# Six LayerNorms of a two-layer decoder: the inverse root moves from ScalarE and VectorE to GpSimd

## The reference

```python
def _layernorm(x, axis=-1, eps=1e-05):
    m = jnp.mean(x, axis=axis, keepdims=True)
    v = jnp.var(x, axis=axis, keepdims=True)
    return (x - m) / jnp.sqrt(v + eps)
...
    x = _layernorm(x + _L0_attn_ref(x, ...), axis=-1)
    x = _layernorm(x + _L0_xattn_ref(x, ctx_2048, ctx_2048, L0_xattn_gamma), axis=-1)
    x = _layernorm(x + _L0_ffn_ref(x, ...), axis=-1)
    x = _layernorm(x + _L1_attn_ref(x, ...), axis=-1)
    x = _layernorm(x + _L1_xattn_ref(x, itok_BxS_13_99985, ...), axis=-1)
    x = _layernorm(x + _L1_ffn_ref(x, ...), axis=-1)
```

## Time and profile before

| | us |
|---|---|
| median of three runs (1048.7 to 1051.43) | 1048.94 |
| the profiled execution's own time | 1048.75 |
| its span, first to last instruction | 1047.0 |
| PE busy in the span | 842.6 |
| DVE busy | 625.5 |
| ACT busy | 439.3 |
| POOL busy | 433.7 |

### The profile page before, as it was taken

The page is one execution under the profiler, slowest core; times in us unless marked ns, Lnnn a source line. Parts: engine busy times, 40 slices in busy tenths (PEclk is TensorE's granted clock), DMA queues, the critical chain, the costliest instruction groups (busy, mean ns, idle before and its releaser), DMA issues. The chain is left out here.

```text
span 1047.0 us, 16284 instructions
## 1 busy us (share of the span) xinstructions
PE 842.6 (80%) x4838; PEld 498.2 (48%) x4838; DVE 625.5 (60%) x1971; ACT 439.3 (42%) x1422; POOL 433.7 (41%) x343
## 2 busy tenths in 40 slices
PE   1959998577475699889999998995994499999920
PEld 0445556344254344355555554883444355555510
DVE  0369994566558477668888887113665633433427
ACT  0038782355156100078888886001112155555512
POOL 0348871244026066556666664000000455565523
PEclk9989998677579699989999999998995599999975
DMA  9200000000000077620000000005911022222114
GB/s 349 108 1 1 0 1 1 0 2 1 0 1 1 17 164 171 141 81 1 2 1 2 1 1 1 1 1 212 317 74 40 16 63 71 73 69 70 51 57 144
DMA packets 30974, 60.44 MB, mean 58 GB/s; under 512 B 6465, under 2 KB 20429, under 8 KB 30032
## 3 DMA queue, kind: packets, MB, share of 16 engines
q1 hardware_dynamic: 17424, 35.99, 10.8%
q10 hardware_dynamic: 8864, 13.00, 4.4%
q0 software_dynamic: 4608, 10.50, 3.2%
HBM read 40.59 MB, written 8.39 MB: 47 GB/s over the span
## 5 line engine op out<-in xcount | busy, mean ns | idle before, releaser
L534 POOL TENSOR_TENSOR a_Pr<-a_Pr,a_rd 128x1024 f32<-128x1024 f32 x64 | 121.3, 1895 | 68.0 <-DVE a_rd L475 67.7
L507 ACT ACTIVATE a_Pr<-a_Sm,a_nm 128x257 f32<-128x257 f32 x256 | 127.3, 499 | 34.2 <-DVE a_nm L459 33.4
L459 DVE CUSTOM_DVE_ANT_0 a_Sm<-a_psS,table,NSK 128x256 f32<-128x256 f32 x256 | 107.7, 477 | 1.8 <-PE a_psS L408 1.8
L408 PE MATMUL a_psS<-KT,QT 64*128 64x256 f32 x512 | 74.2, 410 | 5.7 <-DVE a_nm L459 3.8
L1427 POOL TENSOR_TENSOR ro_in_tile<-ro_in_tile,table 128x384 fp32r<-128x384 f32 x4 | 7.0, 1746 | 173.0 <-DVE ro_in_tile L1486 173.0
L1597 POOL DMA_INDIRECT pairs<-ex_y,ti_index x48 | 49.6, 1034 | 57.5 <-ACT ex_y L1702 56.9
L1110 PE MATMUL p_ps<-p_XT,W 128*128 128x512 f32 x160 | 72.6, 612 | 0.8 <-ACT p_XT L1123 0.8
L408 PEld LDWEIGHTS a_psS<-KT,QT 64*128 64x128 f32 x512 | 45.3, 190 | 57.9 <-issue 48.6
L1140 DVE SCALAR_TENSOR_TENSOR p_T<-p_ps,BQK,table 128x512 f32<-128x512 f32 x80 | 56.4, 746 | 26.7 <-PE p_ps L1110 26.7
L1720 DVE TENSOR_TENSOR ex_a<-ex_psG,ex_sg 128x96 f32<-128x96 f32 x48 | 12.4, 258 | 99.9 <-ACT ex_sg L1690 99.9
L421 PE MATMUL a_psT<-table,a_Pr 128*128 128x128 f32 x512 | 70.8, 282 | 1.5 <-ACT a_PT L514 1.5
(11 more groups left out here) (265 smaller groups left out, 2001.2 us busy)
## 6 DMA issues: line engine op xcount, KB each, us to landing
w_in<-in_w_in SPq DMA_DIRECT2D x1, 6144.0 KB, 18.3
QT<-p_E SPq DMA_DIRECT2D x64, 64.0 KB, 2.1
QT<-p_E ACTq DMA_DIRECT2D x64, 64.0 KB, 2.1
c_in<-in_c_in SPq DMA_DIRECT2D x1, 4096.0 KB, 29.2
co_G<-pairs SPq DMA_DIRECT2D x8, 512.0 KB, 7.5
W<-in_w ACTq DMA_DIRECT2D x1, 3072.0 KB, 16.6
w_out<-in_w_out SPq DMA_DIRECT2D x1, 3072.0 KB, 43.0
KT<-p_E SPq DMA_DIRECT2D x32, 64.0 KB, 2.1
```

What stands on the lines that cost most here:

```text
L408: last = nc.tensor.matmul(psS[:, 2 * (t % 2) + u, qt, :], heads.q(g, n, qt), heads.k(g, n), start=True, stop=True, skip_group_check=True)
L459: nc.vector.tensor_tensor_reduce(out=Sm[:, t % 2, n, 0:S], in0=psS[:, 2 * (t % 2) + n // 2, n % 2, :], in1=mask[:, n % 2, :], scale=-scale ...
L507: nc.scalar.activation(Pr[:, t % 4, n, :], src, ACT.Exp, bias=nm[:, t % 2, n:n + 1], scale=scale if mask is None else -1.0, accum_out=den[ ...
L534: pool.tensor_tensor(p, p, rd[:, t % 2, :].unsqueeze(2).to_broadcast([P, 4, S]), ALU.mult).then_inc(normed, 1)
```

## The change

`Norm.root` is no longer run by ACT but by POOL, as two instructions of 128x8: variance plus epsilon into std, then, behind a wait for its own first instruction, std to the power of a column that holds -0.5 into rstd. Both are tensor_tensor with the second operand a column that is repeated along the row. DVE's reciprocal, and the wait between it and the first normalised tile, go away. The column with -0.5 is a new last column of the constants' table, which is loaded once at the start and grows from 2608 to 2609 columns. Which engine calls `root` is changed in all six users; the rest of the program is the same, but that tiles allocated behind the constants lie 32 bytes further on.

```diff
-    def root(self, act):
-        act.wait_ge(self.has_var, 1)
-        self.nc.scalar.activation(self.std[:, :], self.mv[:, :, 1], ACT.Sqrt,
-                                  bias=self.eps[:, 0:1]).then_inc(self.has_std, 1)
+    def root(self, pool):
+        pool.wait_ge(self.has_var, 1)
+        pool.tensor_tensor(self.std[:, :], self.mv[:, :, 1], self.eps[:, 0:1].to_broadcast([P, NT]),
+                           ALU.add).then_inc(self.has_std, 1)
+        pool.wait_ge(self.has_std, 1)
+        pool.tensor_tensor(self.rstd[:, :], self.std[:, :], self.power[:, 0:1].to_broadcast([P, NT]),
+                           ALU.pow).then_inc(self.has_std, 1)
 
     def apply(self, dve, out):
-        dve.wait_ge(self.has_std, 1)
-        self.chain.link(self.nc.vector.reciprocal(self.rstd[:, :], self.std[:, :]))
+        dve.wait_ge(self.has_std, 2)
...
-        @block.scalar
-        def _(act):
-            ln.root(act)
+        @block.gpsimd
+        def _(pool):
+            ln.root(pool)
...
-             sin0=S, causal=2 * S, window=2 * S, cos1=S, sin1=S, eps=1)
+             sin0=S, causal=2 * S, window=2 * S, cos1=S, sin1=S, eps=1, power=1)
...
-        cos1=cos1, sin1=sin1, eps=np.full((P, 1), EPS))
+        cos1=cos1, sin1=sin1, eps=np.full((P, 1), EPS), power=np.full((P, 1), -0.5))
```

More of the change, by code:

```diff
@@ L557, in __init__ @@
         self.eps = consts["eps"]
+        self.power = consts["power"]
         self.has_var = st.sem(name + "_has_var")
```

## The result

The changed kernel takes 1063.77 us (median of four runs, 1060.85 to 1064.98), the kernel before beside it 1050.18. The ratio is 1.0122 with a 95% interval of 1.0089 to 1.0155: the change makes the kernel slower by about 13 us. The profiled execution is the fastest of the four, 1060.85 us; its span is 1058.8.

A forecast was written before the change was run, and what follows sets the result against it. PE carries most of the span, but short stretches in the six norms with all engines but one idle decide. +5.1 for six norms and -1.28 at a1 sum to +3.8 us: 1052.7 as median, range 1047.5 to 1064.

The forecast's parts named there:

- a power dearer than 1.90 us: Rival: the power costs more than anything POOL does here; at 3 us a norm, +15.5 and 1064.3 us; chance 0.19.
- The six stretches: Last variance to first normalised tile in each norm, other engines idle: 0.61 us becomes 1.46, +0.85 each, +5.1 for six.
- The addition: POOL's 128x8 addition of variance and epsilon in each norm, wholly on the path: 0.20 us.
- the hand-overs: Between engines in each norm: DVE to POOL 0.08 us, POOL to itself 0.08, POOL to DVE 0.05.
- The loads ahead of the roots: Five ACT table loads for the root stand ahead of the wait for the variance: removing them is worth nothing.
- The load at a1: ACT's exponential table load at the second attention's start, behind DVE's first nm, is on the path: removing it gives -1.28 us.
- the rival that rested on it: A table switch costs more than its load, so a1 gains 2.66 us instead of 1.28: 1051.3 us; chance 0.03.
- a first power that pays for its code: Rival: the first power alone is held up by some microseconds, say 6, giving 1058.6 us; chance 0.04.
- The power: POOL's 128x8 power in each norm, on the path: 1.05 us, the middle of 0.20 and 1.90; break-even at 0.41.
- the cheap power: Rival: the power is about as cheap as an addition, 0.41 us or less; at 0.20, 1047.5 us; chance 0.12.
- Whatever is added to or taken from this stretch moves the whole program by as much, six times.: In all six norms DVE has nothing else to do between variance and first tile, so +0.85 us a norm gives +5.1.
- the shifted tiles: Later tiles lie 32 bytes further on: counted as zero, but blamed if a stage between norms ran at another speed.

The follow-up runs named there:

- filled wait: Changed kernel plus five 128x256 matmuls of constants on PE in te, while PE waits for the first tile's gate: 1060.54 us, ratio 1.0124 against the kernel before.
- the wider table: Kernel before with only the 2609th column added to the constants' table, norms as before: 1051.28 us against 1050.03, ratio 1.0011.
- the table loaded ahead: Kernel before plus a one-element exponential on ScalarE in the second projection's block, loading a1's table early: 1047.53 us against 1048.25, ratio 0.9997.
- the version with the filled wait and the early load: Kernel before with tile-by-tile GpSimd power in o0, ff, o1, te, a1's table loaded ahead, five matmuls in te's wait: 1041.17 us against 1050.44.

## Why the prediction was right or wrong

**Direction and range held**: slower, with 1063.77 just inside 1047.5 to 1064. The forecast of 1052.7 was too low, and so was the forecast's own range, which ended at 1057.7. Of the 13 us I had forecast 4. That the range held was luck: its upper part was there for a power dearer than 1.90 us, which did not occur, and two of the four runs lie above it.

**Read rightly.** The six stretches had the form that I described, and nothing hid them. The addition took 0.20 us, the hand-overs 0.08, 0.08 and 0.04, each as read from the rows before. The loads ahead of the roots were worth nothing. The load at a1 was worth 1.3 us in the traces. The first exponential with the load taken away stands where the load had started, so the switch cost 1.28 us and not the 2.66 of the Trainium skill's page ScalarE: Activation LUTs, section What ACT_TABLE_LOAD costs; the rival that rested on it is out. So is the rival of a first power that pays for its code.

**A term of the wrong size.** The power took 1.65 us where I took 1.05, the middle of 0.20 and 1.90. It lay within the bounds, but a middle between two rows that do not show the operation was no estimate, and 6 x 0.60 = 3.6 us hung on it. With 1.65 the sum would have been 6 x 1.44 - 1.28 = +7.4. Of the rivals, the cheap power (0.41 us and less) was wrong by a factor of four or more, and the one dearer than 1.90 us did not occur. The prediction's picture of a power as many operations in one is not tested by any run; they show only the price, 0.16 us for an element where a multiply takes 1.67 ns.

**The step that failed.** "Whatever is added to or taken from this stretch moves the whole program by as much, six times." For five norms together it does, within the noise. For o1 it does not: PE comes back to work behind it in a stage whose start is a few us of work, a wait of 3 us, and work again. With the added 1.45 us the rise of the clock in that start moved from 4.4 to 6.2 us, and two falls came that the kernel before does not have, in the wait and near the end. That cost 5.5 us on top; with the 7.4 us above it makes 12.9 of the 13 us. I had read the clock over the second attention, where it is 1.00, and not in the stages behind a norm, window by window. I had named a stage that runs at another speed as what would make the forecast wrong, but blamed the shifted tiles for it in advance; they do nothing to the time that can be told from the spread.

**What stays open.** What the stage takes goes with the place of the rise. Of the twelve traces without a filled wait, the five with the rise at 4.2 to 4.8 us have no second fall and take 69.3 to 69.6 us. The seven with the rise at 3.8, 5.4, 6.2 (four) and 6.8 us all have one, and take 72.0 to 75.0. What sets the place of the rise was not isolated. It is not the length of PE's idle time alone: with 7.5 us of it the traces have the rise at 4.2 to 4.4 us (three of them), at 3.8 (the wider table), and at 6.8 (the table loaded ahead). Each kernel was traced once, so how often it takes which course is read from the times alone. The extra 1.75 us ahead of o0 were not followed further.

## What to carry to other kernels

Before costing a few tenths of a us on the path between two PE stages, look at PE's granted clock in the stage behind, window by window, in its first 20 us and at its end. Where work, a short wait and work follow each other, 1.5 us added ahead cost 5.5 us on top here, and 3 us added cost none of it. A move of small work off ScalarE to save table loads saves only the loads that a wait does not cover, one of seven here, so price the replacement first, in an idle stretch, at two sizes. And a serial tail that is paid per tensor can be paid per tile while the next tile is made: here it shortened the tail of a norm by 1.9 us. Alone it gained nothing in the whole time, because of the clock; the version with the filled wait and the early load was 9.3 us faster than before.

## What the runs showed of the hardware

- A power on GpSimd (tensor_tensor, float32, 128 partitions) takes 0.37 us and 0.16 us for each element of a partition: 0.58, 0.71, 1.01, 1.63 and 2.89 us at 1, 2, 4, 8 and 16 elements, whether the exponent is -0.5 or 1.0. An addition of 8 elements takes 0.20 us.
- The stage te, the same 160 matmul passes each time, took 69.3 to 69.6 us (five traces), 72.0, 72.6, 74.0, or 74.9 to 75.0 (four), by when PE's clock was at 1.2 GHz in its first 17 us and near its end. Kernels with the same norm ahead of it fell into different ones.
- At 1.2 GHz PE made 5 matmul passes in 3 us where it made 10 at 2.4 GHz.
- A float32 matmul of 128x256 counts as two passes of 0.22 us at the full clock: 24 of them took 10.5 us.
